# Layer 1 attention: sums over products of heads made on TensorE with the identity, two buffers of products, and a new order of steps in all stages

## What is computed

```
def _L1_attn_ref(y_de, Wq, bq, Wk, bk, Wv, bv):
    x = (y_de * mask).reshape(c, t, HEADS, PER_DIM)      # HEADS = 16, PER_DIM = 8
    q = x @ Wq.T + bq
    k_ = x @ Wk.T + bk
    v = x @ Wv.T + bv
    scores = jnp.einsum('cthd,ctgd->cthg', q, k_) * scale
    attn = entmax15(scores, axis=-1)                     # sort, cumulative sums, root, threshold, square
    out = jnp.einsum('cthg,ctgd->cthd', attn, v)
    return out.reshape(c, t, e)
...
x = x + _L1_attn_ref(xn, ...) * _silu(_L1_ffn_ref(xn, ...))
```

## Time and profile before

| what | value |
|---|---|
| median of 3 runs | 3212.63 us (3210.42 to 3227.47) |
| span of the profiled execution, first to last instruction | 3209.0 us |
| busy in the span: PE, DVE, ACT, POOL | 2383.4, 2544.2, 1633.2, 565.8 us |
| mean granted TensorE clock | 0.860 of full |
| first stage ends, second and third stages | at about 1955 us; 1254 us together |

### The profile page before, as it was taken

How to read it: one execution, slowest core, us unless ns; L and a number is a source line. 1 busy time by engine, 2 the same in 40 slices (tenths; PEclk the granted TensorE clock), 3 DMA queues, 4 the chain that set the end, 5 groups by cost and what they waited for, 6 DMA issues and landing times.

```text
span 3209.0 us, 40003 instructions
## 1 busy us (share of the span) xinstructions
PE 2383.4 (74%) x13729; PEld 1300.2 (41%) x13729; DVE 2544.2 (79%) x5554; ACT 1633.2 (51%) x3182; POOL 565.8 (18%) x610
## 2 busy tenths in 40 slices
PE   3697876967958769679674304997688898888888
PEld 1333333333333333334331101332366676666663
DVE  3386898998999999989989673887577777777764
ACT  1344436245344353353442412666587888777862
POOL 0000300302203003012030020001332323323320
PEclk9698987977978879779777655999799999999999
DMA  2001100100101001001010004200688877888751
GB/s 73 1 22 43 30 25 28 35 32 23 34 29 30 26 24 33 28 27 31 30 24 23 23 8 123 57 9 31 198 226 223 235 222 225 220 215 227 220 157 43
DMA packets 270758, 265.92 MB, mean 83 GB/s; under 512 B 15224, under 2 KB 244235, under 8 KB 268987
## 3 DMA queue, kind: packets, MB, share of 16 engines
q1 hardware_dynamic: 270554, 263.37, 28.8%
HBM read 130.48 MB, written 124.45 MB: 79 GB/s over the span
## 4 chain that ended last, share of the span: by engine, by line
DVE 41%; PE 31%; ACT 14%; issue 9%; DMA 2%; POOL 2%; SPq 1%; DVEq 0%; POOLq 0%; ACTq 0%
PE banks L2642 5%; PE banks L2688 4%; DVE t L2618 3%; DVE t L1017 2%; PE banks L2602 2%; DVE t L1169 2%; ACT L144 2%; DVE t L952 1%; ACT t L2629 1%; PE banks L1085 1%; ACT t L2553 1%; DVE t L2673 1%; DVE t L1700 1%; DVE t L1704 1%; ACT t L1395 1%
## 5 line engine op out<-in xcount | busy, mean ns | idle before, releaser
L2618 DVE CUSTOM_DVE_ANT_0 t<-banks,t 128x640 f32<-128x640 f32 (+7 forms) x512 | 377.8, 747 | 135.2 <-PE banks L2642 62.2
L2629 ACT ACTIVATE t<-t 128x640 f32<-128x640 f32 (+7 forms) x512 | 391.0, 780 | 81.3 <-DVE t L2618 80.4
L2642 PE MATMUL banks<-ident,t 128*128 128x128 f32 x2304 | 360.1, 281 | 41.6 <-DVE t L2839 14.4
L2642 PEld LDWEIGHTS banks<-ident,t 128*128 128x128 f32 x2304 | 253.8, 142 | 108.1 <-ACT t L2629 50.5
L2602 PE MATMUL banks<-t 128*128 128x512 bf16 (+3 forms) x768 | 197.3, 333 | 39.4 <-DVE t L2618 37.5
L2583 POOL TENSOR_TENSOR t<-t 128x512 f32<-128x512 f32 x96 | 122.6, 1277 | 551.1 <-DMA t<-relative_scratch 455.7
L548 POOL TENSOR_TENSOR t<-t 128x512 f32<-128x512 f32 x28 | 48.1, 1718 | 915.7 <-ACT t L520 915.7
L2673 DVE COPY t<-banks 128x512 f32<-128x512 f32 x256 | 175.6, 686 | 32.2 <-PE banks L2642 31.3
L1085 PE MATMUL banks<-t 128*128 128x512 f32 x256 | 145.0, 650 | 42.9 <-DVE t L1165 32.3
L1740 ACT ACTIVATE t<-t 128x16 f32<-128x16 f32 x256 | 82.5, 322 | 184.1 <-DVE t L1704 142.4
L1119 ACT ACTIVATE t<-banks 128x512 f32<-128x512 f32 x128 | 76.4, 597 | 195.6 <-PE banks L1085 195.4
(11 more groups left out here) (453 smaller groups left out, 5956.2 us busy)
## 6 DMA issues: line engine op xcount, KB each, us to landing
relative_scratch<-t SPq DMA_DIRECT2D x128, 512.0 KB, 3.6
t<-relative_scratch SPq DMA_DIRECT2D x128, 512.0 KB, 5.2
relative_scratch<-t SPq DMA_DIRECT2D x128, 256.0 KB, 4.1
t<-in_wmoe SPq DMA_DIRECT2D x64, 384.0 KB, 3.0
t<-cut_scratch SPq DMA_DIRECT2D x192, 64.0 KB
t<-t SPq DMA_DIRECT2D x16, 512.0 KB, 4.2
cut_scratch<-t SPq DMA_DIRECT2D x8, 768.0 KB, 4.1
z_scratch<-t SPq DMA_DIRECT2D x8, 512.0 KB, 3.1
```

The source lines that it names most:

```text
L2618: nc.vector.tensor_tensor_reduce(s.s[z][:, 0:n], ps[:, b0:b0 + 1 + i // 4, :].rearrange("p b n -> p (b n)")[:, 0:n], s.bias[r][:, j, WIDE ...
L2629: nc.scalar.activation(s.s[z][:, 0:n], s.s[z][:, 0:n], ACT.Exp, scale=-1.0, bias=s.least[:, z:z + 1]).then_inc(*a.mark("weights", u))
L2642: nc.tensor.transpose(ps[:, 4 + c % 2, (t - lo) * P:(t - lo + 1) * P], s.s[u % NS][:, t * P:(t + 1) * P], k.ident[:]).then_inc(*e.mark("tu ...
```

## The change

It does these things.

1. The reductions at lines 955 and 1020 go (4 and 4 for each unit, 64 in all).
2. The products are laid out with the summed index outermost: 8 slabs of 256 products for the scores, 16 slabs of 128 for the outputs. The columns of the weights of k and v are permuted on the host to match.
3. TensorE sums the slabs. For the scores, for each token block, 8 matmuls with the identity as weights and a slab of 256 columns moving, summed in PSUM (banks S0 + 1 and S0 in turn); ScalarE copies the 256 sums to `o.z` (4 new copies for each unit). For the outputs, 16 matmuls for each token block with a slab as weights and the identity of 128 columns moving, summed in PSUM, so that the sums come out transposed; the transposes of line 897 go.
4. There are two buffers of products; the second takes the place of `o.cum` and `o.cumsq`. VectorE waits for TensorE before it writes products over those of two blocks ago.
5. Heads now lasts, on the shared banks, until the last copy of the scores.
6. The order strings of all engines but POOL are new, in the first stage and in the two others. In the first stage the old strings repeat a pattern from unit to unit; the new ones differ from unit to unit. In the two later stages no instruction is added or removed.

```
 def att1_views(take):
-    o.z, o.cum, o.cumsq = (take((NT, NH * NH)) for _ in range(3))
...
-    o.prod = take((2 * NT * NH * NH,))
-    o.sa, o.sb = (o.prod[:, i * NT * NH * NH:(i + 1) * NT * NH * NH].rearrange("p (t g) -> p t g", t=NT) for i in range(2))
+    o.z, sums = take((NT, NH * NH)), take((2 * NT * NH * NH,))
+    o.cum, o.cumsq = (sums[:, i * NT * NH * NH:(i + 1) * NT * NH * NH].rearrange("p (t g) -> p t g", t=NT) for i in range(2))
...
+    o.prod = [take((2 * NT * NH * NH,)), sums[:, 0:2 * NT * NH * NH]]
...
+SOME = 4
...
 def att1_pe(k, s, u, free):
...
     for t in range(NT):
-        yield
-        for line, *key in free("heads_out", u):
-            pe.wait_ge(line, *key)
-        pe.wait_ge(v, "s_tok", u, t)
-        nc.tensor.transpose(ps[:, bk, t * P:(t + 1) * P], o.s_tok[:, t], k.ident[:]).then_inc(*e.mark("s_tok", u))
+        for d in range(HD):
+            if d % SOME == 0:
+                yield
+                pe.wait_ge(v, "products", u, t)
+                if t >= 2:
+                    pe.wait_ge(a, "z", u, t - 2)
+                elif t:
+                    pe.wait_ge(a, "qkv", u, NT - 1)
+            mm(bank(ps, bk + (t + 1) % 2, NH * NH), k.ident[:], o.prod[t % 2][:, d * NH * NH:(d + 1) * NH * NH], start=(d == 0),
+               stop=(d == HD - 1)).then_inc(*e.mark("z", u, t))
+    for t in range(NT):
+        for g in range(NH):
+            if g % SOME == 0:
+                yield
+                for line, *key in free("heads_out", u):
+                    pe.wait_ge(line, *key)
+                pe.wait_ge(v, "valued", u, t)
+            mm(ps[:, bk, t * P:(t + 1) * P], o.prod[t % 2][:, g * D:(g + 1) * D], k.ident[:], start=(g == 0), stop=(g == NH - 1)).then_inc(
+                *e.mark("s_T", u, t))
 def att1_act(k, s, u):
...
+    for t in range(NT):
+        yield
+        act.wait_ge(e, "z", u, t)
+        nc.scalar.copy(o.z[:, t], bank(ps, bk + (t + 1) % 2, NH * NH)).then_inc(*a.mark("z", u, t))
 def att1_dve(k, s, u):
...
-        tt(prod.rearrange("p (h g d) -> p h g d", h=NH, g=NH), rep(q, 2, NH), rep(kk, 1, NH), ALU.mult).then_inc(*v.mark())
-        yield
-        dve.wait_ge(v)
-        reduce(o.z[:, t], prod.rearrange("p (x d) -> p x d", d=HD), AX, ALU.add).then_inc(*v.mark())
-    yield
+        if t >= 2:
+            dve.wait_ge(e, "z", u, t - 2)
+        elif u:
+            dve.wait_ge(e, "s_T", u - 1, t + 2)
+        else:
+            dve.wait_ge(e, "qkv", u, NT - 1)
+        tt(o.prod[t % 2].rearrange("p (d h g) -> p d h g", h=NH, g=NH), rep(q, 3, NH), rep(kk, 2, NH), ALU.mult).then_inc(
+            *v.mark("products", u, t))
+    yield
+    dve.wait_ge(a, "z", u, NT - 1)
...
-        tt(prod.rearrange("p (h d g) -> p h d g", h=NH, d=HD), rep(w, 2, HD), rep(x, 1, NH), ALU.mult).then_inc(*v.mark())
-        yield
-        dve.wait_ge(v)
-        reduce(o.s_tok[:, t], prod.rearrange("p (x g) -> p x g", g=NH), AX, ALU.add).then_inc(*v.mark("s_tok", u, t))
+        if t >= 2:
+            dve.wait_ge(e, "s_T", u, t - 2)
+        tt(o.prod[t % 2].rearrange("p (g h d) -> p g h d", g=NH, h=NH), rep(w, 3, HD), rep(x, 2, NH), ALU.mult).then_inc(
+            *v.mark("valued", u, t))
...
 def final(k, name, u):
-    return {"ffn0": (k.line("ffn0_act"), "gate", u), "heads": (k.line("att1_act"), "qkv", u, NT - 1),
+    return {"ffn0": (k.line("ffn0_act"), "gate", u), "heads": (k.line("att1_act"), "z", u, NT - 1),
```

More of the change, by code:

```diff
@@ L847, in weights1_dve @@
     for j in range(3):
-        nc.vector.tensor_tensor(s.wqkv[:, j * D:(j + 1) * D], s.wqkv[:, j * D:(j + 1) * D], blocks[:, j // 2], ALU.mult).then_inc(
+        nc.vector.tensor_tensor(s.wqkv[:, j * D:(j + 1) * D], s.wqkv[:, j * D:(j + 1) * D], blocks[:, j % 2], ALU.mult).then_inc(
             *v.mark("all"))
@@ L865, in att1_views @@
     o.qkv = take((NT, 3 * D))
-    o.z, o.cum, o.cumsq = (take((NT, NH * NH)) for _ in range(3))
-    o.s_tok, o.masked = (o.cum.rearrange("p t g -> p (t g)")[:, 0:TB].rearrange("p (t d) -> p t d", t=NT) for _ in range(2))
-    o.prod = take((2 * NT * NH * NH,))
-    o.sa, o.sb = (o.prod[:, i * NT * NH * NH:(i + 1) * NT * NH * NH].rearrange("p (t g) -> p t g", t=NT) for i in range(2))
+    o.z, sums = take((NT, NH * NH)), take((2 * NT * NH * NH,))
+    o.cum, o.cumsq = (sums[:, i * NT * NH * NH:(i + 1) * NT * NH * NH].rearrange("p (t g) -> p t g", t=NT) for i in range(2))
+    o.masked = o.cum.rearrange("p t g -> p (t g)")[:, 0:TB].rearrange("p (t d) -> p t d", t=NT)
+    o.prod = [take((2 * NT * NH * NH,)), sums[:, 0:2 * NT * NH * NH]]
+    o.sa, o.sb = (o.prod[0][:, i * NT * NH * NH:(i + 1) * NT * NH * NH].rearrange("p (t g) -> p t g", t=NT) for i in range(2))
     o.one, o.star, o.tau = take((NT * NH,)), take((NT * NH,)), o.sb
     return o
+SOME = 4
 def att1_pe(k, s, u, free):
@@ L927, in att1_act @@
     yield
-    act.wait_ge(e, "s_tok", u)
+    act.wait_ge(e, "s_T", u, NT - 1)
     if u:
@@ L1810 @@
 TURNS_PE = (
[L1811 to L1820, removed]
@@ new lines @@
+    "aaaaeeaeamaeeeeeeaeaaiiimmmmmmmmmmiimmmmmmmmmiimiiiimmmmmmmmttmmtmmmtmmtmmmtttmggmmmmmeememaaeamaaaaaaaaeaaefmee"
+    "emfeeffeffeffeffeeeeemeffeeeeeemffeefebeeeembeeeeeeeeeeeeeeeemmeaaaaaeeeeaeeemmmmmmmmeemmeeaaaaaaaaaammmmmmmmiim"
+    "imiimmmmmmmmmiimmmmmmimmmimiimmtttttmmttmteegemgaaemaaaaaaaemaaaaefmeeemfeeffefmffmffmeefeeeeeeeeeeeffeeeeeeeeef"
+    "feefebeeeeebeeeeeemmeeeaaaaaaaaeaaaaaaaammmmmmmmeememeeeeeeiiimmmmmmmmmiimmmmmmmmmmmiimmmmmimmmimiimmtttttmmttmt"
+    "eegemgaaemaaaaaaaemaaeaaefemeeefeffefffeffefmeeeemffmffeefeeeeembeeeeeeeeeeeeeebeeeeeeeeeeeeeaaeaeeeaaaaaaeeemem"
@@ new lines @@
+    "aaaaaaammmmmmmmiiimmiimiimmmmmmmmmmmmmmimmmimmiimmmmmmmmmttmmmttmttmteetgemgaaemaaaaaeaeaeeaeaeeemaeeeamfmmmmeee"
+    "eeeeeeeeefeeffefeeeeeffefefeeeefemeemeeeeeeeeeeeffeeeeeefffmmmmmmmmbbaaammaaaaaaaaaammmmmmmmaammaiiimmmmmmmmiimm"
+    "iimmmmmmimmiiimmmtttmmttmtmeetteggaaemaaeaaaaaemaaaaefemeemmeemeefeffefemeffeeffefeeeeeeeeeeffeeeeeeeeffeefeeeee"
+    "ebeeeeebeeaaaaaaaammaaaaaaaaeeeeeeeiiimmmmmmmmiimimimmmmimmmmimmiimmmmmmmmttmmtttmmmtmmmmmttmggmmmmeeeaaeaaaaaaa"
+    "aaaaebeeeeeeeeeeeeeeeeeeeeeeeeeeeeeeeeeeeeeeeeeeeeeeeeeeeeeeeebaaaaaaaaaaaaaaaaiiiiiiiiiiittttttttggbbbb"
@@ new lines @@
+    "stsvtssvstvtstvsststvsstvstsvtstvstssvtssvststvtsvsttssvtssvtststvstvsstsvtsssvttstvtvsssvtstsvstvsvtstvststsvts"
+    "svstststvtssvtsstvsvststvststvsststsvtssvstvtsvtsstsvtssvtstsvtstvstssvtssvtststvstsvtsstsvtsvsstvtsvstsvtsststv"
+    "stsvtvstsstvtsssvtsvtsvtsvtsstsvtssvtststvstsvststvsvststvststvsststsvtssvstsvtvststsvtssvtststvstvsstsvtssvtsts"
+    "tvstsvtsstvsvsstvtststssvtstsvtssvststvtsvtsstsvtsvststvstvstssvststvststvssvtstvstsvststvststssvtstsvtssvstvsts"
+    "vtstsvststsstvststvsttssvtsststsvsttsstsvtv"
@@ L2742 @@
+    "svvstststststvvsstsstsvvtstststvvstssstvvstststvvststssstvvstststvvstsstsvvtstsstststvvsstsstvvstststvvststsssts"
+    "tvvststvvststsvsstvststvsvtststvvvv"
 )
@@ L3341, in laid_out @@
     a.update({
-        "wqkv1": np.concatenate([np.tile(i["L1_attn_W" + k].T, (NH, NH)) for k in "qk"]
-                                + [np.tile(np.repeat(i["L1_attn_Wv"].T, NH, 1), (NH, 1))], 1),
-        "bqkv1": np.concatenate([np.tile(i["L1_attn_b" + k], NH) for k in "qk"] + [np.repeat(i["L1_attn_bv"], NH)])[None, :],
+        "wqkv1": np.concatenate([np.tile(i["L1_attn_Wq"].T, (NH, NH)), np.tile(np.repeat(i["L1_attn_Wk"].T, NH, 1), (NH, 1)),
+                                 np.tile(i["L1_attn_Wv"].T, (NH, NH))], 1),
+        "bqkv1": np.concatenate([np.tile(i["L1_attn_bq"], NH), np.repeat(i["L1_attn_bk"], NH), np.tile(i["L1_attn_bv"], NH)])[None, :],
         "wr1": i["L1_ffn_router_w"],
```

184 lines of the change are left out of this document (86 added, 98 removed).

## The result

The changed kernel takes 3323.1 us (median of 4 runs, 3320.0 to 3326.3). The kernel before takes 3220.1 on the same chip. The ratio is 1.033, 95% interval 1.030 to 1.036: slower by 3.3%, where I had forecast 3% faster.

The account below looks back on a forecast made before the run. VectorE was taken as nearly full, PE close behind. From a 3209.0 us span, -87 (rounds), -6 (ends) and 0 (elsewhere) gave 3116, plus 3.6 from span to median: 3120 us, range 3050 to 3195.

Parts of the forecast that it names:

- The order elsewhere: SP's moved steps and the later stages' new order of the same instructions: 0, range 15 us either way.
- The seven rounds: First stage, heads to heads: each round falls from 215.4 to 203 us, 12.4 less, 87 us for 7.
- The two ends: Last unit loses 17.6 us of reductions, last block's outputs come 4.3 us later: 6 us less taken.
- The later stages: 1254 us after the first stage, PE busy 1064, same instructions in another order: no change taken.
- Time taken from VectorE should therefore show: First-stage round: VectorE busy 94%, no large idle piece, so removing 17.6 us of reductions should shorten it, unless something is just behind.
- the PE demand of 190: PE's work per round in us, which at 91% busy gives the 208 us upper end for the round.
- PE's added work: Score and output sums in each round: 27.0 us at full clock, 54 at half, at 0.43 and 0.22 us a matmul.
- The semaphore increments: On every new matmul: charged nothing; the skill page's 26.3 ns each would add some 2.5 us a round.
- The new waits: VectorE's product waits for PE's sums of two blocks ago: 2 to 6 us idle a round, within the 203.
- Products in their new layout: VectorE's 8 products a round stay at 2.28 us: 0 taken, at most 1.4 us a round.
- ScalarE at nothing: ScalarE's 4 new copies of 0.37 us, 1.5 us a round beside 92.1 busy of 215.4: no cost.
- Rival 3: Longer heads delays the shared banks' hand-over, score sums at half clock: +16 us a round, 3325 us; halfway 3265; chance 0.1.

Follow-up runs that it names:

- Run 3: Changed kernel's sums, first-stage steps laid anew by a longest-chain rule, later stages in the old order, against the kernel before: 3192.8 us, ratio 0.994.
- run 2: Kernel before (VectorE reductions, PE transposes) with its first stage in the changed kernel's order, against the kernel before: 3401.5 us, ratio 1.058.
- first pair of laid orders: First stage laid anew by one rule, against the kernel before: both sums by PE 3192.8 us (0.994), old reductions 3221.6 us (1.002).
- runs 5 and 6: Only the first matmul of each block's sum kept: in the changed kernel with old later orders 3308.7 us (from 3312.5), in Run 3's kernel 3181.3 us (from 3192.8).
- Runs 7 and 9: Second pair of laid orders, same rule with better prices, against the kernel before: both sums by PE 3189.6 us (0.992), no sums by PE 3186.9 us (0.991).

## Why the prediction was wrong

- **The failed step: "The order elsewhere", "I take 0", 15 us either way.** It was priced by PE's idle time in the later stages and by SP's moves, and for the first stage not at all. There the change rewrote every string but POOL's, and that was the largest term of all: -129 us of VectorE's durations against +154 of longer gaps and +76 of dependent steps side by side. Run 3 takes the same arithmetic below the kernel before (3312 to 3193, 119 us by the order), and run 2 puts the old arithmetic far above it (187 us). That the order is the cause is shown; how its loss splits into waits and side-by-side steps is read from one trace of each kernel, and no run changes one of the two alone.
- **The sum, term by term.** The seven rounds were to take 87 us less and took 101 more (1581.8 against 1480.5). The two ends were to give 6 and gave nothing: the first product is 6.4 us later than before, and from the last unit's first product to the copy it is 6.4 us shorter. The later stages were taken at 0 and cost 14.
- **What the rows had said.** VectorE idle 12.8 us of 215.4 with no wait above 2.6 us meant that the old order hid hundreds of short steps between engines. I read it as "VectorE is full, so what is taken off it shows". It was also a sign of how much an order could lose.
- **"Time taken from VectorE should therefore show": half wrong, even under a good order.** I credited 12.4 us a round, from a middle between 197.8 and 208, and the PE demand of 190 behind the 208 has no row. Both sums together gave 29 us over the stage in the first pair of laid orders and nothing in the second. The 64 reductions fell from 146 us to nothing as work, and most of it came back as waits for PE and ScalarE. In the orders that were run only the outputs' half pays.
- **PE's added work: right.** 0.43 and 0.23 us a matmul where I had 0.43 and 0.22, 27 us a round forecast, 23 more busy in the round cut, and nearly free by runs 5 and 6. The clock did what I had said in heads_out, 0.91 in place of 0.58, and the other way in heads, 0.81 in place of 0.92. The rule of the Trainium skill, TensorE: Matmul & The Clock Gate, section The HAM clock gate, that activity releases the clock, agrees with the first: that stretch was filled. The second does not follow from it: PE was busy 42.5 of the 43.8 us of heads, and the clock was at its half level until 1288.3 and again from 1291.7 to 1298.6, though PE had no pause over 0.63 us after 1278.2.
- **The semaphore increments: right.** 4 matmuls with 4 increments in 1.72 us are 0.43 each, just half of a 512-column one. The row shows no extra spacing, so the extra time that the prediction worked out from the Trainium skill's 26.3 ns each is not there.
- **The new waits: at the low end in size, and a small part of the whole.** 12.6 us over 1480 are 1.9 a round where I had said 2 to 6; VectorE's idle time in the round cut was 36.9 us where I had said 14 to 20. The sort's wait on the last copy is small in the changed kernel and shows only when the order is good (22 us).
- **Products in their new layout: right, nothing.** All 64 take 150.1 us against 149.3 (means 2.41 and 2.29 us against 2.39 and 2.28).
- **Later stages:** 14 us, inside my 15.
- **ScalarE at nothing: not quite.** I counted its 4 copies only. The new order also needs 117 table loads in place of 94, 29.5 us more on an engine that VectorE waits for (behind the bar: busy us, mean ns, idle time before them):

```profile
L144 ACT ACT_TABLE_LOAD x117 | 150.1, 1283 | 135.6 <-PE banks L2250 25.8
```

  Runs 7 and 9, with 140 and 138 loads, are faster than the kernel before, so the loads alone decide nothing.
- **Rival 3 had the time (3325) and the wrong cause; that it met the number is luck.** Its half-clock sums in heads were there for the first block only in the round cut, and for 59 of the 512 instructions of the scores' sums in all; the others took 1.72 us for 4 matmuls. Heads did last 23 us longer in the round cut and 14 on average, but run 3 holds the banks as long in rounds of 210.5 us, and run 2 has the slowest rounds with heads as short as before. (Its own halfway number is 3269, not 3265.)

## What to carry to other kernels

Where each engine runs one hand-laid sequence, a change is arithmetic and order, and the order may be the larger term: measure each alone (the old arithmetic in the new order is one run). An engine that is 94% busy may say how good its order is, and not that work taken off it will come out of the time; work that is replaced by a round trip through two other engines can lose where the next step waits for its result. An order laid by one rule is one draw: lay more than one before two kernels are compared by 30 us. When laying steps on one engine, put a step of another chain between two dependent ones.

## What was not expected of the hardware

A VectorE instruction behind its own producer starts 0.03 us after the end of that one; an independent one starts some 0.09 before it (0.72 and 0.60 us from start to start for 512 elements, above). The new order has 582 more such starts, and 76 us more in the column of short gaps. The Trainium skill, VectorE: DVE Perf Modes, section The DRAIN you can't avoid, says of eight copies with a semaphore after each that the semaphore costs nothing extra; the rows of this kernel show 0.12 us where the next instruction has to wait for it.

VectorE and GpSimd get in each other's way. In the kernel before, VectorE's timeline (start, duration, instruction):

```profile
471.15 0.69 DVE L610 TENSOR_TENSOR t<-t 128x512 f32<-128x512 f32 x1 [0.94 <-ACT t L520]
471.76 1.48 DVE L611 TENSOR_TENSOR t<-t 128x256 f32<-128x256 f32 x1
```

And GpSimd's:

```profile
471.19 1.77 POOL L548 TENSOR_TENSOR t<-t 128x512 f32<-128x512 f32 x1 [20.79 <-ACT t L520]
```

In the kernel before, line 611 takes 1.48 to 1.49 us in the 25 of its 32 executions that start inside GpSimd's line 548, and 0.41 to 0.42 in the other 7; it ends 0.28 us after the GpSimd instruction. In the changed kernel only 4 start so, and other lines are hit in its place. There are 28 of these GpSimd instructions, and beside them VectorE instructions lose 28 us in the kernel before and 26 in the changed one, so this is no part of the difference.
